# Normalising the first head group's attention output during the second group's projection, with the inverse row sums spread by DMA

## What is computed

```python
qkv = einsum('oc,bchw->bohw', w_qkv, x)
q, k, v = split(qkv, 3, axis=1)                     # each (b, 8, 32, 4096)
scores = einsum('bhdi,bhdj->bhij', q, k) / sqrt(32)
attn = softmax(scores, axis=-1)
out = einsum('bhij,bhdj->bhdi', attn, v)
x = einsum('oc,bchw->bohw', w_proj, out) + x        # end of layer 0
# layer 1: theta, phi, g are 1x1 convolutions of this x; softmax(theta^T phi) g; W; batch norm; + x
```

## Time and profile before

| | us |
|---|---|
| median of 3 runs | 2544.92 |
| lowest, highest | 2544.74, 2545.19 |
| the profiled execution | 2545.51 |
| its span | 2543.4 |

### The profile page before, as it was taken

The page is one execution under the profiler, slowest core; times in us unless marked ns, Lnnn a source line. Parts: engine busy times, 40 slices in busy tenths (PEclk is TensorE's granted clock), DMA queues, the critical chain, the costliest instruction groups (busy, mean ns, idle before and its releaser), DMA issues.

```text
span 2543.4 us, 62417 instructions
## 1 busy us (share of the span) xinstructions
PE 2456.2 (97%) x27050; PEld 784.6 (31%) x27054; DVE 2151.0 (85%) x1354; ACT 2263.9 (89%) x2510; POOL 455.4 (18%) x652
## 2 busy tenths in 40 slices
PE   7999999989999999999999999999899999999998
PEld 3222222242222222344442222222422222223443
DVE  6899999878999999895578999999689999898954
ACT  7999999979999999566489999999799999994663
POOL 0222222202222222110002222222022222220100
PEclk9999999999999999999999999999999999999999
DMA  3777777726777777301237777777177777771011
GB/s 112 146 147 141 146 145 143 146 46 138 143 147 145 142 146 144 60 1 71 82 75 146 143 145 147 143 142 142 40 145 142 147 146 142 145 144 27 1 59 42
DMA packets 94287, 296.12 MB, mean 116 GB/s; under 512 B 18640, under 2 KB 19728, under 8 KB 93744
## 3 DMA queue, kind: packets, MB, share of 16 engines
q0 software_dynamic: 73728, 268.47, 52.7%
q1 hardware_dynamic: 20288, 23.72, 2.9%
HBM read 14.75 MB, written 8.68 MB: 9 GB/s over the span
## 4 chain that ended last, share of the span: by engine, by line
PE 87%; ACT 8%; DVE 3%; issue 1%; DMA 0%; POOL 0%; ACTq 0%; SPq 0%; DVEq 0%
PE psOL L435 36%; PE psOL L424 27%; PE psOL L834 7%; ACT arena L508 4%; PE scores L298 3%; ACT arena L507 3%; PE scores L733 2%; DVE arena L548 2%; PE psOL L760 1%; PE psOL L402 1%; PE psOL L410 1%; PE scores L424 1%; PE scores L309 1%; PE scores L821 1%; PE scores L822 1%
## 5 line engine op out<-in xcount | busy, mean ns | idle before, releaser
L548 DVE TENSOR_TENSOR arena<-arena 128x2048 f32<-128x2048 f32 x736 | 1686.3, 2291 | 109.2 <-ACT arena L508 53.5
L508 ACT ACTIVATE arena<-scores 128x1536 f32<-128x1536 f32 x1024 | 1561.6, 1525 | 0.0
L435 PE MATMUL psOL<-arena 128*32 128x512 f32 (+1 forms) x11264 | 1074.0, 484 | 1.4 <-ACT arena L508 1.4
L424 PE MATMUL psOL<-arena 32*128 32x512 f16 x3072 | 839.5, 379 | 37.5 <-ACT arena L507 34.7
L424 PE MATMUL scores<-arena 32*128 32x512 f16 x9216 | 846.6, 379 | 0.0
L507 ACT ACTIVATE arena<-psOL 128x512 f32<-128x512 f32 x1024 | 676.8, 661 | 14.5 <-PE scores L424 14.5
L574 POOL DMA_DIRECT2D arena<-arena x448 | 387.6, 889 | 1136.5 <-ACT arena L508 830.0
L424 PEld LDWEIGHTS psOL<-arena 32*128 32x128 f16 x3072 | 206.7, 92 | 850.6 <-ACT arena L507 724.1
L435 PEld LDWEIGHTS psOL<-arena 128*32 128x32 f32 x11264 | 270.8, 108 | 522.2 <-issue 426.7
L424 PEld LDWEIGHTS scores<-arena 32*128 32x128 f16 x9216 | 220.5, 92 | 0.0
L834 PE MATMUL psOL<-arena 128*128 128x512 f16 x768 | 170.3, 379 | 0.0
(11 more groups left out here) (113 smaller groups left out, 1334.3 us busy)
## 6 DMA issues: line engine op xcount, KB each, us to landing
arena<-arena POOLq DMA_DIRECT2D x512, 512.0 KB, 5.3
X<-in_x SPq DMA_DIRECT2D x16, 512.0 KB, 4.6
out<-arena SPq DMA_DIRECT2D x32, 256.0 KB, 2.0
arena<-pool_inv SPq DMA_DIRECT2D x2, 2048.0 KB, 7.9
arena<-in_w_qkv SPq DMA_DIRECT2D x1, 768.0 KB, 4.4
Ls<-L SPq DMA_DIRECT2D x32, 8.0 KB
att_inv<-Ls SPq DMA_DIRECT2D x32, 8.0 KB
arena<-in_W_w SPq DMA_DIRECT2D x2, 256.0 KB, 2.7
```

The costliest lines, as they stand in the source:

```text
L424: last = nc.tensor.matmul(dst[h], K[rows, kp, j * 128:(j + 1) * 128], Q[rows, qp, cs], start=(n == 0), stop=(n == 2))
L435: last = nc.tensor.matmul(both[h * D:(h + 1) * D, lo:hi], V[:, j, h * D:(h + 1) * D], P[:, r + h, lo:hi], start=(j == 0), stop=(j == JT - 1))
L508: nc.scalar.activation(P[:, r + 1:r + G, :], bank[n % 2].rearrange("p (u n) -> p u n", n=CH), ACT.Exp, scale=SCORE).then_inc(s_exp, 1)
L548: nc.vector.tensor_tensor(acc[:], old, P[:, r:r + G, :], ALU.add).then_inc(s_add, 1)
```

## The change

Group 0's output for chunks 0 to 6 is multiplied by the inverse sums in `project[1]`. SP, once it has seen that group 0's sums of all chunks are done (`SUMS * NC`), issues two DMAs that read the 4 rows of `att_inv` and write each 32 times, onto all 128 partitions, into `Rf` at 88 to 102 KB of `arena`, that is slots 5 and 6 of the ring: chunks 0 to 2 first, then 3 to 6, each with its own semaphore. VectorE multiplies chunk c-1 at the end of its turn c. ScalarE waits ahead of its step 5 of the second group's attention until all seven products are done, since that step writes slot 5. In the second layer TensorE spreads, and VectorE multiplies, only group 1 for chunks 0 to 6; chunk 7 keeps both groups. The PSUM targets alternate, so `broadcast(c)` waits for an older product.

```diff
+SUMS = 2
+FIRST_ROWS = [(0, 3), (3, NC - 1)]
...
+        Rf = view(88 * KB, (1, 1, (NC - 1) * CH))[:, 0, 0]
...
-            def vector(dve, between):
+            def spread_first(sp, b):
+
+                sp.wait_ge(attend[0].signals["sum"], SUMS * NC)
+                for k, (lo, hi) in enumerate(FIRST_ROWS):
+                    cs = slice(lo * CH, hi * CH)
+                    sp.dma_start(Rf[:, cs], r_dram[b, 0:G, cs].unsqueeze(1).broadcast_to([G, D, (hi - lo) * CH])
+                                 ).then_inc(s_rf[k], 16)
+
+            def normalise_first(dve, c):
+                cs = slice(c * CH, (c + 1) * CH)
+                dve.wait_ge(s_rf[sum(1 for lo, hi in FIRST_ROWS if hi <= c)], 16)
+                nc.vector.tensor_tensor(O[:, 0, cs], O[:, 0, cs], Rf[:, cs], ALU.mult).then_inc(s_nf, 1)
+
+            def vector(dve, between, first=False):
...
                     if c >= 2:
                         largest(c - 1)
+                    if c and first:
+                        normalise_first(dve, c - 1)
...
-            def scalar(act):
+            def scalar(act, emptied):
                 for n in range(NC * JT):
                     r = n % RING * G
                     act.wait_ge(s_ready, n + 1)
+                    if n == 5 and emptied:
+                        act.wait_ge(*emptied)
...
+            def groups_of(c):
+
+                return range(NG) if c == NC - 1 else [1]
+
             def spread_to(c):
 
-                return psOL if c else scores6[:, 4 * CH:6 * CH]
+                return slot(5) if c == 0 else psOL if c == NC - 1 else (psO, psL)[c % 2]
...
-                    pe.wait_ge(s_rc[rows_of(c)], 16 * NG)
-                    if c:
+                    pe.wait_ge(s_rc[rows_of(c)], 16 * len(groups_of(c)))
+                    if c == NC - 1:
                         pe.wait_ge(s_norm, c)
+                    elif c >= 3:
+                        pe.wait_ge(s_norm, c - 1)
...
-                    for g in range(NG):
+                    for n, g in enumerate(groups_of(c)):
                         rows = slice(32 * g, 32 * g + G)
-                        last = nc.tensor.matmul(spread_to(c)[:, g * CH:(g + 1) * CH], spread[rows, :],
+                        last = nc.tensor.matmul(spread_to(c)[:, n * CH:(n + 1) * CH], spread[rows, :],
                                                 Rr[rows, c * CH:(c + 1) * CH], start=True, stop=True)
...
-                    nc.vector.tensor_tensor(O[:, :, cs], O[:, :, cs],
-                                            spread_to(c).rearrange("p (g n) -> p g n", n=CH), ALU.mult
+                    part = O[:, NG - len(groups_of(c)):NG, cs]
+                    nc.vector.tensor_tensor(part, part, spread_to(c).rearrange("p (g n) -> p g n", n=CH), ALU.mult
                                             ).then_inc(s_norm, 1)
...
-                    attend[0].scalar(act)
+                    attend[0].scalar(act, None)
                     project[1].scalar(act, None, attend[0].signals["room"], None)
-                    attend[1].scalar(act)
+                    attend[1].scalar(act, (project[1].signals["nf"], NC - 1))
...
-                    project[1].vector(dve, attend[0].vector_end)
+                    project[1].vector(dve, attend[0].vector_end, True)
...
                     attend[0].sync(sp, b)
+                    project[1].sync(sp, b)
```

More of the change, by code:

```diff
@@ L279, in projection @@
             s_ve = sem(root, f"s_ve_{g}")
+            s_rf = [sem(root, f"s_rf{k}_{g}") for k in range(len(FIRST_ROWS))]
+            s_nf = sem(root, f"s_nf_{g}")
             def both_units(c):
@@ L1114, in rows @@
                     cs = slice(ROWS[k] * CH, ROWS[k + 1] * CH)
-                    for g in range(NG):
+                    for g in groups_of(ROWS[k]):
                         sp.dma_start(Rr[32 * g:32 * g + G, cs], r_dram[dram, g * G:(g + 1) * G, cs]).then_inc(s_rc[k], 16)
```

8 lines of the change are left out of this document (4 added, 4 removed).

## The result

| kernel | median us | lowest to highest | runs |
|---|---|---|---|
| before | 2544.54 | 2543.57 to 2545.19 | 6 |
| changed | 2556.19 | 2552.55 to 2559.90 | 6 |

The changed kernel takes 1.0045 times as long (95% interval 1.0034 to 1.0057), 11.6 us more. The forecast was 2.3 us less, and the measured time lies above its range. The profiled execution of the changed kernel took 2559.9 us, with a span of 2557.6.

A forecast was written before the change was run, and what follows sets the result against it. TensorE was taken to bound the second layer, and a chain through VectorE part of the second projection. Removed 6.9 us, added 4.6: net 2.3 us faster, 2542.6 us, range 2537.3 to 2547.5.

The forecast's parts named there:

- What bounds the kernel: TensorE sets the second layer's 5.99 us turn; in the second projection, chunks 3 and 4 go through VectorE, ScalarE, TensorE.
- Removed, 6.9 us: Second layer: group 0's spread matmuls for chunks 1 to 6 go, saving 3.2 us and 3.7 us in the two images.
- Two groups cost 1.06 us, one costs half, 0.53 us: Second layer's turn on TensorE: leaving out one of the two spread matmuls was to save 0.53 us.
- VectorE's products: Second projection: seven added products of 0.6 us each fall into VectorE's idle time, costing 0 to 0.1 us.
- the exponential's wait: ScalarE's new wait ahead of its sixth exponential comes after all seven products, so it costs nothing.
- the second DMA: Chunks 3 to 6: lands near 552.8, ahead of its first product due at about 554.4, so it costs nothing.
- Added, 2.5 + 2.1 = 4.6 us: Second projection: VectorE's wait for the first new DMA delays the chain by 2.5 and 2.1 us in the two images.
- 532.35 + 9.65: First new DMA, first image: issued at 532.35, landing 9.65 us later at 542.0, carried by four engines.
- the pool_inv broadcast: One row onto 128 partitions at 378 GB/s, share 0.90; taken to give four engines 94 to 105 GB/s.
- Rival 4: Second layer does not shorten because VectorE's chain takes over in a turn: 4.6 us slower, 2549.5 us; chance 0.03.
- Rival 3: The two DMAs share four engines packet by packet, so the first lands with the second: 2565 us; chance 0.10.
- Rival 2: Half clock behind TensorE's gaps or at the second layer's entry moves the time by over 1.5 us; chance 0.28.

The follow-up runs named there:

- the kernel with one spread matmul: Kernel before, with group 0's spread matmul left out for chunks 0 to 6 and no DMA or product added: 2545.16 us, ratio 0.9996.
- the one with the two apart: Kernel before, with the chunk's first output matmuls set between the two groups' spread matmuls from chunk 2 on: 2559.04 us, ratio 1.0055.
- three kernels that have all of them: Changed kernel with one DMA a head (ratio 0.9999), with products two chunks later (1.0000), or with seven DMAs of one chunk each (1.0001).
- kernel with three pieces: Changed kernel, with the spread DMA in three pieces of 1, 2 and 4 chunks instead of two of 3 and 4: 2556.70 us, ratio 1.0045.
- the kernel with the second piece held back: Changed kernel, with the second spread DMA issued only when the first has landed: 2570.57 us, ratio 1.0093.

## Why the prediction was wrong

**What bounds the kernel: right.** TensorE sets the turn of the second layer, with no gap, and the third and fourth chunks of the second projection go through VectorE. The waits landed just where that chain says.

**Removed, 6.9 us: wrong, it is 0.** The step that failed is "Two groups cost 1.06 us, one costs half, 0.53 us". One costs 1.06, as the kernel with one spread matmul and the one with the two apart both show. The same view could have told: in the earlier trace rows the four spread records take 1.13 us, 0.28 each, while the eight full ones of the output projection take 3.70, 0.46 each. Records of the same 512 columns in the same type that come out cheaper than full ones were the sign that they overlap.

**VectorE's products, the exponential's wait, the second DMA: right.** Seven products at 0.60 us cost nothing once their operands are there (ratios 0.9999 to 1.0001 in three kernels that have all of them), and the fourth product of the changed kernel has no wait. The kernel with three pieces shows that the last point held only because the first wait had made everything late.

**Added, 2.5 + 2.1 = 4.6 us: the mechanism right, the size wrong, it is 5.7 + 6.3 = 12.0.** Four engines, VectorE's queue behind the wait, ScalarE's square, no recovery: all as forecast. Of the 12.0 us, 5.6 + 5.2 are the late square, 3.1 more in each image than forecast, and about 1.1 is TensorE at half clock behind its gap. The term that was mis-sized is the landing, "532.35 + 9.65": it took 12.8 us from the issue and not 9.65, the 3.1 us. The traffic went at 55 and then 75 GB/s where I took 94 to 105, worked out from the pool_inv broadcast, and its end is ragged. The pool_inv row bounded 16 engines on a 2 MB transfer; it was no bound for four on a smaller one. The other row that I had, the copy of L, gave 25 GB/s at a share of 0.21; I used its share and left its rate aside.

The sum of the two errors, 6.9 + 7.4 = 14.3, takes the forecast of -2.3 to +12.0; the medians differ by 11.6, the spans of the two profiled executions by 14.2.

**The rivals.** Rival 4 (no shorter turn, 0.03) had the right outcome for the second layer by a wrong reason: VectorE's chain did not take over, it had 0.9 us to spare in the one-matmul turn (5.98 less 5.07). Rival 3 (shared engines, 0.10) named the size of a late landing from which the kernel gets slower; the landing was 2.9 us later, but not by sharing, as the kernel with the second piece held back shows. Rival 2 (the clock, 0.28): the gap in TensorE's work was there, and in the kernel with three pieces, behind the wait of 4.59 us, the granted clock was 0.50 for 6 us (558 to 564). In the changed kernel itself it was 0.50 from 1810 to 1816 and cost 1.0 us in the second image; three kernels without the wait were at full clock from 1808 to 1816. So the clock took part, as this rival said, but its share is small. The way into the second layer moved too, by 1.1 us in the first image, which is within what the executions differ there. The chance of 0.12 for slower was too low because both mistaken terms were held by one reading each, and neither had a bound on the other side: the removed term's other end was 0.

## What to carry to other kernels

Before a matmul is counted as a share of its neighbours' time, multiply the records by their mean and divide by the busy time of the line. Here 1.2 to 1.3 is what matmuls that follow one another show, and 2.3 was the sign of a pair that runs side by side; removing one of such a pair may remove nothing. Here one was worth 0, and both 18 us. A DMA that something waits for must be judged by the date of each part: cut it into the pieces that are needed in turn, put more rows outermost where it is urgent (with 32 in place of 4 the share went from 0.25 to about 1 here), and ask for each piece when it will be due once the wait ahead of it is gone.

## What the runs showed of the hardware that I had not expected

- A matmul of 4 rows by 512 columns in f32 holds TensorE for 1.05 us alone and the pair on different rows for 1.06. Without both the turn is 1.25 us shorter.
- Four DMA engines at the same share of about 0.25 moved 55 to 98 GB/s in the changed kernel, low at the start of a transfer and higher later, and 98 with seven small DMAs queued. What sets the rate is open.
- The last bytes of a single DMA moved at an ever smaller share, 0.18 and then 0.06 in the 4 us before it landed, so the four engines did not end together.
- Behind a gap of 4.1 us in TensorE's work the granted clock was 0.50 for some 6 us, and 1.00 at the same place (1808 to 1816) in three kernels without the gap.
